# First cross-attention of a two-layer decoder: softmax sums from TensorE to VectorE and GpSimd

## What is computed

```python
q = q.reshape(B, Lq, H, hd).transpose(0, 2, 1, 3)      # x @ Wq + bq, H = 16, hd = 8
...
q = _larope(q, Lq)
k = _larope(k, Lk)
scores = jnp.einsum('bhqd,bhkd->bhqk', q, k) * SCALE
scores = jnp.where(context_mask[:, None, None, :], scores, -jnp.inf)
attn = jax.nn.softmax(scores, axis=-1)                 # over 77 keys
out = jnp.einsum('bhqk,bhkd->bhqd', attn, v)
out = out.transpose(0, 2, 1, 3).reshape(B, Lq, H * hd)
return out @ Wo + bo                                   # then x = x + this
```

## Time and profile before

| | before |
|---|---|
| median of 3 runs | 1526.28 us (1521.62 to 1527.96) |
| the profiled execution, its own time | 1520.3 us |
| its span, first to last instruction | 1518.5 us |
| PE busy in the span | 1376.9 us, 91% |
| DVE busy | 1028.1 us, 68% |
| ACT busy | 717.3 us, 47% |
| POOL busy | 541.3 us, 36% |
| this stage, from its first scores to the last addition | 514.6 to 616.0 us |

### The profile page before, as it was taken

How to read it: one execution, slowest core, us unless ns; L and a number is a source line. 1 busy time by engine, 2 the same in 40 slices (tenths; PEclk the granted TensorE clock), 3 DMA queues, 4 the chain that set the end, 5 groups by cost and what they waited for, 6 DMA issues and landing times.

```text
span 1518.5 us, 29647 instructions
## 1 busy us (share of the span) xinstructions
PE 1376.9 (91%) x11068; PEld 977.6 (64%) x11068; DVE 1028.1 (68%) x2477; ACT 717.3 (47%) x1467; POOL 541.3 (36%) x548
## 2 busy tenths in 40 slices
PE   6999999999999699526999899899999999979998
PEld 4677677677677366313576576667666666648887
DVE  3777777777776777785133386877978886766554
ACT  2666666666666365101033155455555454524222
POOL 1555555555555000103412374442333333211110
PEclk7999999999999799757999899999999999999999
DMA  3331000000000200000132224111211211000000
GB/s 126 84 102 34 2 1 2 1 1 2 1 1 1 63 2 1 1 0 9 40 101 54 47 85 96 34 37 45 39 33 50 40 27 30 20 1 1 1 0 28
DMA packets 74551, 47.23 MB, mean 31 GB/s; under 512 B 25817, under 2 KB 65578, under 8 KB 74422
## 3 DMA queue, kind: packets, MB, share of 16 engines
q1 hardware_dynamic: 71798, 44.00, 11.0%
q0 software_dynamic: 2048, 1.27, 0.3%
q10 hardware_dynamic: 576, 0.20, 0.1%
HBM read 21.63 MB, written 10.49 MB: 21 GB/s over the span
## 4 chain that ended last, share of the span: by engine, by line
PE 75%; DVE 18%; ACT 3%; issue 2%; ACTq 0%; DMA 0%; SPq 0%; POOL 0%; DVEq 0%
PE psum L1080 8%; PE psum L1067 8%; PE psum L1057 7%; PE psum L1455 7%; PE psum L1569 6%; PE psum L1446 5%; PE psum L1580 4%; PE psum L1467 4%; PE psum L1440 3%; DVE negmax L2129 3%; PE psum L1282 2%; PE psum L1034 2%; PE psum L1087 2%; PE psum L1045 2%; PE psum L1002 2%
## 5 line engine op out<-in xcount | busy, mean ns | idle before, releaser
L568 POOL TENSOR_TENSOR arena<-arena,rden 128x512 f32<-128x512 f32 x256 | 260.8, 1040 | 211.5 <-DVE rden L1680 211.5
L747 ACT ACTIVATE arena<-psum,negmax 128x512 f32<-128x512 f32 x256 | 174.8, 691 | 148.3 <-DVE negmax L1671 139.5
L1671 DVE TENSOR_REDUCE negmax<-psum 128x1 f32<-128x512 f32 x256 | 168.2, 682 | 71.7 <-PE psum L1057 71.7
L2129 DVE TENSOR_REDUCE negmax<-psum 128x1 f32<-128x512 f32 x256 | 165.0, 685 | 63.2 <-PE psum L1446 61.9
L1067 PEld LDWEIGHTS psum<-cst,arena 128*128 128x128 f32 x1024 | 113.5, 140 | 41.1 <-issue 40.5
L1067 PE MATMUL psum<-cst,arena 128*128 128x128 f32 x1024 | 136.7, 276 | 0.9 <-DVE w L1666 0.4
L1446 PE MATMUL psum<-w,wqkv 128*64 128x208 f32 x1024 | 122.6, 362 | 0.0
L625 POOL TENSOR_TENSOR a_qblk<-a_qstack,cst 96x512 fp32r<-96x512 f32 x64 | 68.7, 1073 | 140.6 <-PE psum L1446 131.3
L1057 PE MATMUL psum<-a_qk 64*128 64x512 f32 x768 | 107.1, 411 | 2.5 <-DVE a_qk L1689 2.5
L927 ACT ACTIVATE kT<-psum,negmax 128x512 f32<-128x512 f32 x64 | 43.9, 687 | 128.5 <-PE psum L1455 71.9
L1569 PE MATMUL psum<-f_h,f_w 128*128 128x512 f32 x384 | 99.8, 409 | 1.8 <-DVE arena L2258 1.7
(11 more groups left out here) (323 smaller groups left out, 2811.1 us busy)
## 6 DMA issues: line engine op xcount, KB each, us to landing
a_kstack<-a_khi SPq DMA_DIRECT2D x128, 64.0 KB, 2.0
w<-in_ew SPq DMA_DIRECT2D x2, 2048.0 KB, 8.5
a_kstack<-a_klo SPq DMA_DIRECT2D x64, 64.0 KB, 2.0
xs_rows<-f SPq DMA_DIRECT2D x3, 1024.0 KB, 5.4
arena<-xs_rows SPq DMA_DIRECT2D x8, 384.0 KB, 3.6
ys_rows<-wqkv SPq DMA_DIRECT2D x8, 384.0 KB, 2.6
a_qstack<-a_qhi SPq DMA_DIRECT2D x120, 16.0 KB, 1.8
q_by_row<-qtok SPq DMA_DIRECT2D x4, 256.0 KB, 2.5
```

What stands on the lines that cost most here:

```text
L568: pool.tensor_tensor(a0_p[u % 4], a0_p[u % 4], rden[:, u:u + 1].broadcast_to([P, SEQ]), ALU.mult).then_inc(a0_norm, 1)
L747: act.activation(a0_p[u % 4], bank[u % 4][:, :], ACT.Exp, bias=negmax[:, u:u + 1], accum_out=den[:, u:u + 1]).then_inc(a0_exp, 1)
L1671: dve.tensor_reduce(negmax[:, u:u + 1], bank[u % 4][:, :], AX.X, ALU.max, negate=True).then_inc(a0_max, 1)
L2129: dve.tensor_reduce(negmax[:, n % 8:n % 8 + 1], bank[n % 4][:, :], AX.X, ALU.max, negate=True).then_inc(a1_max, 1)
```

## The change

The sums of the exponentials leave PE. `x0_denominators(t)` is now a DVE function: it sums the 77 exponentials of each head (1232 to 16) in SBUF and takes the reciprocal of the 16 sums. GpSimd then multiplies the tile's 1232 exponentials with these reciprocals, in place, before PE transposes them. The matmuls with ones and the block of ones are gone, and so are the reciprocal over 256 columns and the product with it: `x0_feats(u)` is a plain copy from PSUM. There are three buffers `x0_p` in place of two and `x0_shifted`; DVE writes the shifted scores into one of them and ACT takes the exponential in place. PE runs the scores two tiles ahead of the transposes (before: one), and the loop on DVE takes the sums of tile t-1 after the shift of tile t. Two matmuls of `keep_busy` near the end of the stage are gone.

```diff
@@ -211,11 +211,9 @@
...
 x0_vz = big_k_flat[0:LK, B * HQ * LK:B * HQ * LK + B * VZ].rearrange("p (b c) -> p b c", b=B)
-x0_one = big_k_flat[0:LK, B * HQ * LK + B * VZ:B * HQ * LK + B * VZ + 7 * HD]
-x0_p = [wqkv0[:, i * H * LK:(i + 1) * H * LK] for i in range(2)]
-x0_shifted = wqkv0[:, 2 * H * LK:3 * H * LK]
+x0_p = [wqkv0[:, i * H * LK:(i + 1) * H * LK] for i in range(3)]
 x0_f = featsT[:, 0:UQ]
-x0_rden = featsT[:, UQ:2 * UQ]
+x0_rden = [featsT[:, UQ + i * H:UQ + (i + 1) * H] for i in range(2)]
 x0_pT = [arena[0:LK, 2 * i:2 * i + 2, :, :].rearrange("p a b c -> p (a b c)").rearrange("p (h q) -> p h q", h=H) for i in range(2)]
...
@@ -552,9 +549,6 @@
...
     pool.memset(x0_vz, 0.0).then_inc(setup, 1)
-    pool.memset(x0_one, 0.0).then_inc(x0_ones, 1)
-    pool.wait_ge(x0_ones, 1)
-    pool.memset(x0_one[:, 3 * HD:4 * HD], 1.0).then_inc(x0_ones, 1)
 
...
@@ -566,6 +560,11 @@
...
             pool.tensor_tensor(a0_p[u % 4], a0_p[u % 4], rden[:, u:u + 1].broadcast_to([P, SEQ]), ALU.mult).then_inc(a0_norm, 1)
+
+    for t in range(NT):
+        pool.wait_ge(x0_rd, t + 1)
+        p = x0_p[t % 3].rearrange("p (h k) -> p h k", h=H)
+        pool.tensor_tensor(p, p, bcast(x0_rden[t % 2], 2, LK), ALU.mult).then_inc(x0_unit, 1)
 
...
@@ -788,25 +787,23 @@
...
         if t >= 4 and c == 0 and t % 2 == 0:
-            act.wait_ge(x0_den, t // 2 - 1)
+            act.wait_ge(x0_num, t // 2 - 1)
         act.activation(x0_pT[t // 2 % 2][:, c * HQ:(c + 1) * HQ, t % 2 * P:(t % 2 + 1) * P],
...
         act.wait_ge(x0_sub, t + 1)
-        if t >= 2:
-            act.wait_ge(x0_t, t * 4 - 4)
-        act.activation(x0_p[t % 2], x0_shifted, ACT.Exp).then_inc(x0_exp, 1)
+        act.activation(x0_p[t % 3], x0_p[t % 3], ACT.Exp).then_inc(x0_exp, 1)
 
     x0_exp_of(0)
-    for t in range(1, NT):
+    x0_exp_of(1)
+    for t in range(2, NT + 2):
         for c in range(2):
-            x0_copy(t - 1, c)
-        x0_exp_of(t)
+            x0_copy(t - 2, c)
+        if t < NT:
+            x0_exp_of(t)
         for c in range(2, 4):
-            x0_copy(t - 1, c)
-    for c in range(4):
-        x0_copy(NT - 1, c)
+            x0_copy(t - 2, c)
 
...
@@ -1140,7 +1137,6 @@
...
     pe.wait_ge(pre_pool, 4)
-    pe.wait_ge(x0_ones, 2)
 
...
@@ -1160,14 +1156,14 @@
...
         if c == 0:
-            pe.wait_ge(x0_exp, t + 1)
+            pe.wait_ge(x0_unit, t + 1)
         if t == 0 and c == 0:
...
             mm = pe.transpose(bank[4 + c % 2][0:LK, j * P:(j + 1) * P],
-                              x0_p[t % 2][:, (c * 4 + j) * LK:(c * 4 + j + 1) * LK], ident)
+                              x0_p[t % 3][:, (c * 4 + j) * LK:(c * 4 + j + 1) * LK], ident)
         mm.then_inc(x0_t, 1)
...
@@ -1184,13 +1180,6 @@
...
 
-    def x0_denominators(u):
-        for i in range(HQ):
-            for j in range(4):
-                mm = pe.matmul(bank[6][32 * j:32 * j + 32, UQ:2 * UQ], x0_one[:, (3 - i) * HD:(7 - i) * HD],
-                               x0_pT[u % 2][:, 4 * j + i, :], start=(i == 0), stop=(i == HQ - 1))
-        mm.then_inc(x0_den, 1)
-
     def x0_output(u):
...
@@ -1202,25 +1191,21 @@
...
     x0_scores(0)
-    for t in range(1, NT + 4):
+    x0_scores(1)
+    for t in range(2, NT + 4):
         if t < NT:
             x0_scores(t)
-        if t <= NT:
-            x0_turn_t(t - 1, 0)
-            x0_turn_t(t - 1, 1)
-        u = (t - 3) // 2
-        if t % 2:
-            if u == NT // 2:
-                keep_busy(bank[0], 2)
-            if 0 < u <= NT // 2:
-                x0_output(u - 1)
-            if 0 <= u < NT // 2:
-                x0_numerators(u)
-        elif 0 <= u < NT // 2:
-            x0_denominators(u)
-        if t <= NT:
-            x0_turn_t(t - 1, 2)
-            x0_turn_t(t - 1, 3)
+        if t < NT + 2:
+            x0_turn_t(t - 2, 0)
+            x0_turn_t(t - 2, 1)
+        u = (t - 4) // 2
+        if t % 2 == 0 and 0 <= u < NT // 2:
+            x0_numerators(u)
+        if t % 2 == 1 and 0 <= u < NT // 2:
+            x0_output(u)
+        if t < NT + 2:
+            x0_turn_t(t - 2, 2)
+            x0_turn_t(t - 2, 3)
 
...
@@ -1749,17 +1734,23 @@
...
         ln(dve.tensor_reduce(mx0[:, :].rearrange("p (j i) -> p j i", j=4), s, AX.X, ALU.max))
-        if t:
-            dve.wait_ge(x0_exp, t)
-        dve.tensor_tensor(x0_shifted.rearrange("p (j i k) -> p j i k", j=4, i=HQ), s,
+        if t >= 3:
+            dve.wait_ge(x0_t, t * 4 - 8)
+        dve.tensor_tensor(x0_p[t % 3].rearrange("p (j i k) -> p j i k", j=4, i=HQ), s,
                           bcast(mx0[:, :].rearrange("p (j i) -> p j i", j=4), 3, LK), ALU.subtract).then_inc(x0_sub, 1)
 
-    def x0_normalise(u):
-        dve.wait_ge(x0_den, u + 1)
-        ln(dve.reciprocal(x0_rden, bank[6][:, UQ:2 * UQ]))
+    def x0_denominators(t):
+        dve.wait_ge(x0_exp, t + 1)
+        if t >= 2:
+            dve.wait_ge(x0_unit, t - 1)
+        ln(dve.tensor_reduce(x0_rden[t % 2], x0_p[t % 3].rearrange("p (h k) -> p h k", h=H), AX.X, ALU.add))
+        dve.reciprocal(x0_rden[t % 2], x0_rden[t % 2]).then_inc(x0_rd, 1)
+
+    def x0_feats(u):
+        dve.wait_ge(x0_num, u + 1)
         if u:
             dve.wait_ge(x0_o, u)
-        dve.tensor_tensor(x0_f, bank[6][:, 0:UQ], x0_rden, ALU.mult).then_inc(x0_norm, 1)
+        dve.tensor_copy(x0_f, bank[6][:, 0:UQ]).then_inc(x0_norm, 1)
 
...
@@ -1776,11 +1767,13 @@
...
             x0_shift(t)
+        if 1 <= t <= NT:
+            x0_denominators(t - 1)
         if t == 1:
...
         if t % 2 == 0 and 0 <= u < NT // 2:
-            x0_normalise(u)
+            x0_feats(u)
         if t % 2 and 0 <= u < NT // 2:
```

More of the change, by code:

```diff
@@ L312, in decoder_kernel @@
         setup = sem("setup")
-        x0_ones = sem("x0_ones")
         ln_step, ln_stat, ln_mean_ok, ln_var_ok, ln_std_ok, ln_ready, ln_tp, ln_out = (
@@ L323, in decoder_kernel @@
             sem("a0_" + n) for n in ("ql", "kl", "qc", "kc", "vc", "exp", "max", "rd", "tcd", "tca", "norm", "ftc", "x"))
-        x0_q, x0_qr, x0_s, x0_sub, x0_exp, x0_t, x0_tc, x0_num, x0_den, x0_norm, x0_o, x0_x = (
-            sem("x0_" + n) for n in ("q", "qr", "s", "sub", "exp", "t", "tc", "num", "den", "norm", "o", "x"))
+        x0_q, x0_qr, x0_s, x0_sub, x0_exp, x0_t, x0_tc, x0_num, x0_rd, x0_unit, x0_norm, x0_o, x0_x = (
+            sem("x0_" + n) for n in ("q", "qr", "s", "sub", "exp", "t", "tc", "num", "rd", "unit", "norm", "o", "x"))
         g_mm, g_chain, g_exp, g_pool, b_chain, b_count, b_total = (
```

## The result

In the comparison on one chip the kernel before took 1523.95 us (median of 4 runs, 1520.82 to 1527.96), the changed one 1536.24 us (4 runs, 1533.28 to 1544.53). The ratio is 1.008, with a 95% interval of 1.0051 to 1.0108: slower by 12.3 us, where the forecast was slower by 12.6 and 1539 us.

What follows compares the result with a forecast made beforehand. PE was the bound before; changed, a loop of waits through GpSimd, PE and DVE sets 11.9 us a pair. +7.6 at held clock and +5 for clock falls make +12.6 on 1526.3: 1539 us, range 1530 to 1549.

Steps and rivals of the forecast that it cites:

- The loop through GpSimd, PE and DVE: From an even tile's reciprocals through product, PE's queue and DVE to those two tiles later: 11.9 us per pair against 11.09.
- the loop of the odd tiles: Same chain of waits for odd tiles, with the output (1.57 us) in the numerators' place (1.87): 11.6 us.
- Rival 1: Faster: busy time alone decides in the stage, 10.3 us per pair, 1522 us in all; chance 0.06.
- Rival 2: PE's clock holds in the stage, so only the 7.6 us are added: 1534 us (1530 to 1536); chance 0.24.
- Rival 3: Same time: loop and DVE some 5% shorter, start and end hide more; 1523 to 1530 us; chance 0.10.
- the line through the earlier trace: GpSimd's product, from two rows with a repeated operand: 1.66 ns per column plus 191 ns, 2.24 us for 1232 columns.
- Rival 4: GpSimd's product takes 2.5 to 2.78 us, the loop grows 0.3 to 0.5 per pair: 1543 to 1552 us; chance 0.10.
- The sum at full clock: Stage with the clock held at 1.00: start +2.4, middle +3.5, end +1.7, together +7.6 us.
- middle: Five pairs of the stage, from the shift of tile 4 to that of tile 14: taken as +3.5 us.
- the walk: Going through the stage queue by queue with the same durations: start +2.4, middle +2.9, end +1.7 us.
- The clock: PE's granted clock falls five or six times over the stage, 0.9 us for each of six: +5 us, 0 to +12.
- one wait of 2.5 to 2.7 us, once per pair: PE idles ahead of an even tile's transposes, 2.5 to 2.7 us per pair, so its clock falls in most pairs.

Runs made afterwards that it cites:

- the kernel with filler: The changed kernel with added matmuls that nobody reads in PE's waits of this stage: stage 106.6 us, 1.0057 and 1.0041 times the kernel before in two sets of runs.
- the second group: Set of runs on one chip that repeated the changed kernel unaltered: median 1553.56 us against 1526.16 for the kernel before, ratio 1.0153.

## Why the prediction was right

**What bounds the kernel.** Right. The loop through GpSimd, PE and DVE closed, at 11.77 us where 11.93 was forecast; the loop of the odd tiles has 11.36 (reciprocals at 579.79 and 591.15), forecast 11.6:

```profile
579.79 0.25 DVE L1747 RECIPROCAL featsT<-featsT 128x16 f32<-128x16 f32 x1
...
591.15 0.25 DVE L1747 RECIPROCAL featsT<-featsT 128x16 f32<-128x16 f32 x1
```

Rival 1, busy time alone, fell: it is what the kernel without the product does, 9.84 a pair and 92.9 for the stage. Its condition was mis-stated: with product, hand-overs and PE's part at 6.5 us the loop would take 6.5 + 4.6 = 11.1, the pair of before; for 10.3 they would have to come to 5.7. Rival 2, the clock that holds, is what the kernel with filler does. Rival 3, a loop 5% shorter, fell with the 11.77.

**Product and sums.** The product took 2.247 us against 2.24 from the line through the earlier trace rows, 1.82 ns per column with the fixed part in it. The prediction's estimate of 2.8 us from the Trainium skill (GPSIMD Engine Reference, section 3.1) doesn't hold for this product with a repeated operand; the measurement decides. Rival 4 fell with that. Sums took 1.43 by duration and 1.46 by starts, against 1.48. The hand-over from GpSimd to PE took 0.05 us (588.25 - 585.95 - 2.25) and not 0.15, which is most of what the loop is shorter.

**The sum at full clock.** +6.7 by the kernel with filler, forecast +7.6: start 2.5 for 2.4, middle 2.7 for 3.5, end 1.5 for 1.7. The middle is the term that was too large: the walk had given 2.9, and I had raised it towards five times 0.8, which counts the first pairs as if they had no lead.

**The clock.** +6.8 in this execution, forecast +5, within 0 to 12; in the execution of the second group +19.2, outside it, and with it that group's median, 1553.56 us, is outside the forecast's 1530 to 1549. The size came out near, the picture did not, and that the medians differ by 12.3 us where 12.6 was forecast is in part luck: in the stage +6.7 and +6.8 stand in place of +7.6 and +5. I had the falls spread evenly, in most pairs. In the kernel after, the clock fell once in the middle and cost 1.0 us there; 5.8 of the 6.8 us are the start and the end. The step that failed is "one wait of 2.5 to 2.7 us, once per pair". The waits for the product from 571 to 590, in turn of an odd and an even tile, are

```profile
571.05 1.10 PE L1165 MATMUL psum<-cst,wqkv 128*77 128x128 f32 x8 [1.57 <-POOL wqkv L567]
...
576.50 1.10 PE L1165 MATMUL psum<-cst,wqkv 128*77 128x128 f32 x8 [1.08 <-POOL wqkv L567]
...
582.42 1.10 PE L1165 MATMUL psum<-cst,wqkv 128*77 128x128 f32 x8 [1.17 <-POOL wqkv L567]
```

The fourth is 1.47, at 588.25 (above). The sum per pair is 2.64 to 2.65, as forecast (1.57 + 1.08 and 1.17 + 1.47), but the odd tiles have part of it. The share of the even tiles grows from pair to pair (1.08, 1.47, 1.87) and that of the odd ones shrinks (1.57, 1.17, 0.77), by the 0.4 us that the odd loop is shorter. Behind these shorter waits the clock held. In the second group's execution the even tiles had most of it (2.47, 1.71, 2.10, 2.71, 2.67), and the clock fell behind three of these five (the first, third and last). That the share of the wait decides between the two is my reading; no run fixed it by itself. The rule quoted from the Trainium skill, that a PE which idles briefly between groups loses its clock again and again, agrees with both traces (granted clocks of 0.90 and 0.91, 0.73 and 0.78 from 530 to 560 and from 560 to 590); how often, it doesn't say.

**The end.** A wait of 3.4 us was forecast ahead of the last transposes of an even tile; it was 3.03, and the clock was low for the 10 us around and behind it (the row in order of time, and the busy times of the stretch):

```profile
611.78 1.99 PE L1165 MATMUL psum<-cst,wqkv 128*77 128x128 f32 x8 [3.03 <-POOL wqkv L567]
```

```profile
610.00:620.00 10.00, 8.21 (x52) 5.42 (x53) 2.09 (x5) 2.38 (x5) 3.94 (x2) 0.50 0.01 2
```

PE is busy 8.21 of these 10 us at half its clock, and little else runs: what the clock takes here isn't hidden, 4.0 us in all.

**Behind the stage** the profiled executions differ by 0.5 us, within the 3 of the forecast; for the kernel with filler it was 6.1 (909.0 against 902.9), so 3 is too narrow for a kernel like this one.

## What to carry to other kernels

When a new step is put between two engines, walk once round the queues: add up from the new step through everything that stands ahead of what it indirectly feeds, and divide by the tiles that the loop spans. Here that sum, forecast at 11.9 and measured at 11.8, decided, while every engine had under 10 us of work per pair. Where the loop is the bound, move the feeding work ahead of the waiting work (here the scores, by one tile and one buffer) before making any step faster: that gave back 1.8 us a pair, where halving the new step gave 1.0. And this kernel, in which PE waits in every pair, did not have one time but two, 1536 and 1554 us: look at more than one execution before reading a per cent.

## What the runs showed that was not expected

**One kernel, two stages.** The changed kernel, unaltered, had a stage of 113.4 us in two profiled executions and of 125.8 in a third, at 1.008, 1.009 and, for the third, 1.015 times the kernel before beside it. What makes it start on one course or the other stays open.

**DVE beside GpSimd.** The fourth product of the rotation of q, of two operands in SBUF, took 1.61 us in the kernel after. At that place it took 0.69 in the kernel before, and 0.69 in the kernel without the product on GpSimd; then the kernel after:

```profile
524.59 0.69 DVE L1746 TENSOR_TENSOR big_q<-big_q,x0buf 128x512 f32<-128x512 f32 x1
```

```profile
525.68 0.69 DVE L1726 TENSOR_TENSOR big_q<-big_q,x0buf 128x512 f32<-128x512 f32 x1
```

```profile
524.93 2.25 POOL L567 TENSOR_TENSOR wqkv<-wqkv,featsT 128x1232 f32<-128x1232 f32 x1 [35.92 <-DVE featsT L1747]
...
526.12 1.61 DVE L1731 TENSOR_TENSOR big_q<-big_q,x0buf 128x512 f32<-128x512 f32 x1
```

GpSimd's product ran from 524.93 to 527.18, over the first 1.06 us of it; the product itself kept its 2.25. DVE's sum and subtraction, with one large operand each, show nothing of the kind beside the same product (1.42 us for the sum at 609.60, 1.44 for the subtraction at 533.55). The Trainium skill (SBUF — State Buffer, section on who interferes with whom) says that a DVE instruction with two SBUF inputs and a GpSimd instruction that reads SBUF can't go on together, and that the second to start waits until the first ends. The row agrees: by that rule it would have ended at 527.18 + 0.69 = 527.87, and it ended at 527.73. The runs bear it out further: it took 0.69 us in the two kernels of before and in the one without the product, 1.61 in every kernel with the whole product, and 1.75 in the three with the product in halves. It comes once per launch, at the start of the stage, and plays no part in the loop.
